# Graph layer kernel: the second join adds the base rows on GpSimd, and the last node stage reads one sum and stores the norms alone

## What is computed

```
xn = _layernorm(x, axis=-1)
x = x + _L0_gnn_ref(xn, edge_index, edge_attr_16, ...) + _L0_mix_ref(xn[None], ...)[0]
x = x + _L0_ffn_ref(_layernorm(x, axis=-1)[None], ...)[0]
return x
```

## Time and profile before

| | us |
|---|---|
| three runs | 3036.64, 3046.49, 3049.08 |
| median | 3046.49 |
| the profiled execution | 3039.37 |
| its span in the trace | 3037.6 |

### The profile page before, as it was taken

The page is one execution under the profiler, slowest core; times in us unless marked ns, Lnnn a source line. Parts: engine busy times, 40 slices in busy tenths (PEclk is TensorE's granted clock), DMA queues, the critical chain, the costliest instruction groups (busy, mean ns, idle before and its releaser), DMA issues. The chain is left out here.

```text
span 3037.6 us, 76113 instructions
## 1 busy us (share of the span) xinstructions
PE 2343.2 (77%) x15555; PEld 1937.5 (64%) x15556; DVE 2164.0 (71%) x6024; ACT 1172.0 (39%) x4767; POOL 1995.0 (66%) x2241
## 2 busy tenths in 40 slices
PE   6587878888888887847777777777777757499897
PEld 4466667676666666636666666666666536378786
DVE  7477878787877786647777778777787655666565
ACT  3244545444444444513333333333333442322222
POOL 4577777777777774577777777777777225166665
PEclk9799989999999999859988989898888857699999
DMA  9755655565555553256566556655555248444432
GB/s 255 207 169 156 172 157 166 166 171 160 166 168 168 157 167 86 86 146 180 159 178 175 168 169 175 176 167 173 172 169 167 62 140 271 121 160 152 122 116 86
DMA packets 295113, 484.48 MB, mean 159 GB/s; under 512 B 69669, under 2 KB 204989, under 8 KB 295045
## 3 DMA queue, kind: packets, MB, share of 16 engines
q0 software_dynamic: 96384, 286.92, 33.3%
q1 hardware_dynamic: 134340, 150.23, 17.1%
q10 hardware_dynamic: 64320, 46.56, 4.9%
HBM read 404.17 MB, written 81.43 MB: 160 GB/s over the span
## 5 line engine op out<-in xcount | busy, mean ns | idle before, releaser
L703 POOL DMA_INDIRECT e_rows<-table,e_idx x1664 | 1580.2, 950 | 557.1 <-issue 403.4
L1087 PE MATMUL e_ps_sum<-e_hot,e_msg 128*128 128x129 f32 x6656 | 1118.6, 306 | 267.3 <-DVE e_msg L744 210.6
L1087 PEld LDWEIGHTS e_ps_sum<-e_hot,e_msg 128*128 128x128 f32 x6656 | 920.9, 205 | 427.0 <-ACT parts L942 242.2
L941 ACT ACTIVATE acc<-e_ps_sum 128x256 f32 x1664 | 639.0, 384 | 1222.8 <-PE e_ps_sum L1087 1022.7
L744 DVE TENSOR_TENSOR e_msg<-e_rows,e_ps_pr 128x256 f32<-128x256 f32 x1664 | 654.6, 415 | 82.0 <-issue 12.9
L723 DVE TENSOR_TENSOR e_hot<-e_ps_pr,rel 128x512 f32<-128x512 f32 x416 | 285.4, 686 | 163.2 <-PE e_ps_sum L1087 157.7
L1069 PE MATMUL e_ps_al<-e_dst_score,e_hotT 128*128 x3328 | 301.6, 180 | 1.5 <-issue 0.7
L1069 PEld LDWEIGHTS e_ps_al<-e_dst_score,e_hotT 128*128 128x128 bf16 x3328 | 251.5, 99 | 60.1 <-issue 2.3
L942 ACT ACTIVATE parts<-e_ps_sum 128x4 f32 (+1 forms) x1664 | 280.4, 168 | 0.0
L1076 PE MATMUL e_ps_al<-ident,e_lr 128*128 128x128 f32 x104 | 38.6, 371 | 171.8 <-DVE e_lr L768 170.8
L2010 ACT ACTIVATE x_h<-x,eb 128x128 f32<-128x128 f32 x216 | 67.4, 363 | 260.8 <-PE x L2079 260.8
(11 more groups left out here) (319 smaller groups left out, 3400.4 us busy)
## 6 DMA issues: line engine op xcount, KB each, us to landing
e_relb<-rel_rows SPq DMA_DIRECT2D x104, 512.0 KB
e_rows<-table,e_idx POOLq DMA_INDIRECT x1664
e_eattr<-in_edge_b SPq DMA_DIRECT2D x104, 128.0 KB
e_xT<-turned_x ACTq DMA_DIRECT2D x100, 128.0 KB
e_xr<-in_x ACTq DMA_DIRECT2D x100, 128.0 KB
node<-acc SPq DMA_DIRECT2D x25, 512.0 KB, 3.8
table<-t_row SPq DMA_DIRECT2D x25, 276.0 KB, 4.1
table<-j_row SPq DMA_DIRECT2D x25, 276.0 KB, 2.5
```

Of the source, the lines that this page charges most:

```text
L703: nc.gpsimd.indirect_dma_start(out=rows[q][:, k, :], out_offset=None, in_=table, in_offset=bass.IndirectOffsetOnAxis(ap=idx[:, q, k:k + 1] ...
L941: nc.scalar.activation(acc[:, :, bass.ds(at[k], P)], ps_sum[(k + q) % 3][:, :, 0:P], ACT.Copy).then_inc(s["window"], 1)
L1087: op = nc.tensor.matmul(ps_sum[(k + q) % 3][:, a, 0:WIN], msg[:, k % RM, a * P:a * P + P], hot[:, q, k, :], start=(a == 0), stop=True, ski ...
```

## The change

The second join's result goes to the first 256 columns of `node` (row width 528) and no longer to a tensor `conv`, and what is stored there is already the sum with `base`:

- SyncE fetches the chunks of `base` into a new ring `part` of four, the first four ahead of all and then chunk n + 4 behind the store of chunk n.
- GpSimd adds `part` to `row` (128 x 512) behind each row copy. The store waits for this add.
- The base rows of the fix nodes are gathered by seven indirect DMAs at the head of GpSimd's program. VectorE adds them to `fix`, six blocks in one instruction and the last in another, and the scatters wait for these.

In `front` SyncE fetches one chunk of `node` straight into a slot of `xy`, now a ring of six (RX). There is no add. The fetch of chunk n + 4 is issued behind the store of chunk n and waits for the landing of the store of chunk n - 2. The store writes the second half of a slot only, 256 KB.

```diff
+            def fetch(n, q):
+                if layer == 1:
+                    sp.dma_start(part[:, q], base[bass.ds(n * CH, CH), :].rearrange("(b p) f -> p b f", p=P)
+                                 ).then_inc(s[f"part{q}"], 16)
...
+                for q in range(RR):
+                    store(RR * i + q, q)
+                    fetch(RR * i + RR + q, q)
...
+            if layer == 1:
+                def add(n, q, i):
+                    pool.wait_ge(s["rowc"], n + 3)
+                    pool.wait_ge(s[f"part{q}"], 16 * i + 16)
+                    pool.nop(nofuse=True)
+                    nc.gpsimd.tensor_tensor(row[:, q], row[:, q], part[:, q], ALU.add).then_inc(s["split"], 1)
+
+                for f in range(NFIX):
+                    n = min(P, T - f * P)
+                    nc.gpsimd.indirect_dma_start(
+                        out=fix_part[0:n, f, :], out_offset=None, in_=base,
...
+            else:
+                f, n = NFIX - 1, T - (NFIX - 1) * P
+                vec.wait_ge(s["fix_part"], 16 * NFIX)
+                vec.wait_ge(s["fixc"], f)
+                nc.vector.tensor_tensor(fix[:, 0:f], fix[:, 0:f], fix_part[:, 0:f], ALU.add).then_inc(s["fixs"], 1)
...
             def fetch(n):
-                if n >= 4:
-                    sp.wait_ge(s["x2"], n - 3)
-                sp.dma_start(bb[:, n % 4], base[n * CH:n * CH + CH, :].rearrange("(b p) f -> p b f", p=P)).then_inc(s[f"b{n % 4}"], 16)
-                sp.dma_start(cb[:, n % 4], conv[n * CH:n * CH + CH, :].rearrange("(b p) f -> p b f", p=P)).then_inc(s[f"c{n % 4}"], 16)
...
+                if n >= RX:
+                    sp.wait_ge(s[f"o{n % RX}"], 16 * (n // RX))
+                    sp.wait_ge(s["yt"], n - RX + 1)
+                sp.dma_start(xy[:, n % RX, :, 0:F], node[n * CH:n * CH + CH, 0:F].rearrange("(b p) f -> p b f", p=P)
+                             ).then_inc(s[f"x{n % RX}"], 16)
...
-                sp.dma_start(node[n * CH:n * CH + CH, 0:2 * F].rearrange("(b p) f -> p b f", p=P), xy[:, n % 3]
-                             ).then_inc(s[f"o{n % 3}"], 16)
...
+                sp.dma_start(node[n * CH:n * CH + CH, F:2 * F].rearrange("(b p) f -> p b f", p=P), xy[:, n % RX, :, F:2 * F]
+                             ).then_inc(s[f"o{n % RX}"], 16)
+                if n + RX - 2 < NCH:
+                    fetch(n + RX - 2)
...
-            for n in range(NCH + 1):
-                if n < NCH:
-                    pool.wait_ge(s[f"b{n % 4}"], 16 * (n // 4) + 16)
-                    pool.wait_ge(s[f"c{n % 4}"], 16 * (n // 4) + 16)
-                    if n >= 3:
-                        pool.wait_ge(s[f"o{n % 3}"], 16 * (n // 3))
-                        pool.wait_ge(s["yt"], n - 2)
-                    nc.gpsimd.tensor_tensor(xy[:, n % 3, :, 0:F], bb[:, n % 4], cb[:, n % 4], ALU.add).then_inc(s["x2"], 1)
```

More of the change, by code:

```diff
@@ L134, in build @@
             join(nc, sb, pb, sem, locals())
-        node = nc.dram_tensor("node", (NP, MW), F32).ap()
         mid = nc.dram_tensor("mid", (NP, MW), F32).ap()
@@ L1209, in join @@
     begins, sep, same = v["begins"], v["ends_sep"], v["ends_same"]
-    result = v["table"][1] if layer == 0 else v["conv"]
+    result = v["table"][1] if layer == 0 else v["node"]
+    base = v["base"]
     WIDTH = TW if layer == 0 else F
@@ L1248, in store @@
             def store(n, q):
-                sp.wait_ge(s["split" if layer == 0 else "rowc"], n + (1 if layer == 0 else 3))
-                sp.dma_start(result[bass.ds(n * CH, CH), :].rearrange("(b p) f -> p b f", p=P), row[:, q]
+                sp.wait_ge(s["split"], n + 1)
+                sp.dma_start(result[bass.ds(n * CH, CH), 0:WIDTH].rearrange("(b p) f -> p b f", p=P), row[:, q]
                              ).then_inc(s[f"out{q}"], 16)
-            with sp.Fori(0, ROUNDS) as i:
+            def fetch(n, q):
+                if layer == 1:
+                    sp.dma_start(part[:, q], base[bass.ds(n * CH, CH), :].rearrange("(b p) f -> p b f", p=P)
+                                 ).then_inc(s[f"part{q}"], 16)
+            for q in range(RR):
+                fetch(q, q)
+            with sp.Fori(0, ROUNDS - 1) as i:
                 for q in range(RR):
                     store(RR * i + q, q)
+                    fetch(RR * i + RR + q, q)
+            for q in range(RR):
+                store(NCH - 1 - RR + q, q)
+                if q == 0:
+                    fetch(NCH - 1, 0)
             store(NCH - 1, 0)
@@ L1272, in _ @@
                 nc.gpsimd.tensor_tensor(qs[:, 2, :], qs[:, 1, :], cst[:, 1:2].broadcast_to((P, NB)), ALU.pow)
+            if layer == 1:
+                def add(n, q, i):
[7 more added lines that the diff above has]
+                        out=fix_part[0:n, f, :], out_offset=None, in_=base,
+                        in_offset=bass.IndirectOffsetOnAxis(ap=fix_rows[0:n, f:f + 1], axis=0)).then_inc(s["fix_part"], 16)
+                with pool.Fori(0, ROUNDS) as i:
+                    for q in range(RR):
+                        add(RR * i + q, q, i)
+                add(NCH - 1, 0, ROUNDS)
             for q in range(RR):
@@ L1491, in front @@
     ident, cst, logits = v["ident"], v["cst"], v["logits"]
-    base, conv, node = v["base"], v["conv"], v["node"]
+    node = v["node"]
+    RX = 6
     with ExitStack() as ctx:
@@ L1514, in front @@
         ps_l = pb("f_l", [P, 512], ctx)
-        names = ("small", "b0", "b1", "b2", "b3", "c0", "c1", "c2", "c3", "o0", "o1", "o2", "x2", "mv", "rstd", "yn", "yt", "ytc",
+        names = ("small", *(f"x{q}" for q in range(RX)), *(f"o{q}" for q in range(RX)), "mv", "rstd", "yn", "yt", "ytc",
                  "rh", "rhc", "lg")
@@ L1554, in _ @@
+            for n in range(NCH):
+                pool.wait_ge(s["mv"], n + 1)
+                nc.gpsimd.tensor_tensor(rstd[:, n % 2], eps[:, n % 2], cst[:, 0:1].broadcast_to((P, 2)), ALU.pow
+                                        ).then_inc(s["rstd"], 1)
         @block.vector
```

35 lines of the change are left out of this document (15 added, 20 removed).

## The result

| | before | after |
|---|---|---|
| median, us | 3043.43 (4 runs, 3036.64 to 3049.08) | 3015.16 (4 runs, 3012.53 to 3016.59) |
| profiled execution, span | 3037.6 | 3010.7 |
| second join, VectorE's first scan to first scatter | 63.65 | 81.62 |
| last node stage, first fetch to logits | 102.84 | 58.22 |

The ratio is 0.9899, 95% interval 0.9884 to 0.9913: 28.3 us less, where 3017 and faster was forecast. The change is small, 1%, but the interval lies clear of 1. The spans differ by 26.9 us, and they add up: -2.5 (the join's first scan comes earlier), +18.0 (the join), +0.6 (scatters), -44.6 (the last node stage), +1.6 (all behind it).

A forecast was written before the change was run, and what follows sets the result against it. The prediction took the last node stage's three-deep ring as the limit there; front -43.1 and second join +15.7 give -27.4 us, from 3044.1 to about 3017 us, range 2999 to 3039.

The forecast's parts named there:

- Lock: Second join: GpSimd adds and VectorE scans block each other for the other's length; plus 15.7 us, without it only 3.1.
- tail: Second join's end: first scatter needs six copied fix rows and a VectorE add, not one copied row; 3.1 us more.
- The walk: Second join traced over the earlier rows, one add entering each gap between VectorE instructions: first scatter 15.7 us later.
- The gathers ... Nothing: Second join's start: seven gathers at 1.3 us take 9 us, done before the first row is copied; no cost.
- SyncE ... Nothing: Second join: 25 fetch issues of some 0.4 us in an almost empty queue, four rows ahead; no cost.
- L: Front: length of the first low-clock stretch, taken as 14 us; 25 steps take 46.8 + 0.46 L, 53.2 us.
- TensorE becomes the bound wherever the clock is low: Front: a TensorE step takes 3.47 us at the low clock, 1.87 at the high one, against VectorE's 1.87.
- the ring of three: Front before: a slot's store, landing, add, power and normalisation take 7.3 us for two steps and limit the stage.
- just hidden: Front: fetch landing of about 3 us plus 0.6 of issues is 3.6 against 3.74 us for two steps.
- B: Rival, second join: the adds hide, join +3.1 us, total change -40.0, 3004 us; chance 0.12.
- C: Rival, front: clock low for all 25 steps, front 93.3 us, total change +6.2, 3050 us; chance 0.14.
- D: Rival, front: fetch landing stays 4.2 us, a step 2.4, front 68.9, total change -18.2, 3026 us; chance 0.14.

The follow-up runs named there:

- no adds: Changed kernel without GpSimd's 25 adds in the second join, fetches and gathers kept: join 67.65 us, last row copied 59.21 us in, whole 3007.7 us.
- fills: Changed kernel with each of GpSimd's 25 second-join adds replaced by a fill of a scratch buffer that reads nothing: join 69.22 us, ratio to before 0.9900.
- the four profiles above: Unedited join profiled four times, once with the last node stage's fetch three steps ahead: 81.5 to 81.6 us three times, 79.08 us once.
- six slots: Kernel before with only the ring xy of the last node stage deepened from three slots to six: front 94.15 us, whole 3032.0 against 3046.3 us.
- The two other profiles with three held gathers: Two of the three unedited-join profiles near 81.6 us, with gathers held 4.04 to 4.21, 3.38 and 1.69 us.
- the pair of kernels: Changed kernel with TensorE adding base rows behind transposes, either both transposes of a bank opening a group or only the first: joins 67.66 and 67.74 us.

## Why the prediction held, and where its steps did not

**The total** was right within 2 us (3017 against 3015.2), and -27.4 for the profiled span against -26.9. Terms in it are wrong in ways that cancel, within `front` above all, so the closeness of the total is in part luck. So is the first scatter at 2489.89 where 2490.1 was forecast: the join's first scan came 2.5 us earlier than before.

**Join, +15.7 forecast, +18.0 and +15.4 measured.** Lock right in kind (no adds: 67.65; fills: 69.22). By place: L1479 +6.6 as forecast; last row +12.5 forecast, +14.0 and +11.4 measured; tail 3.1 forecast, 4.0 measured, so it was short by 0.9, since the fix copies come one behind the other before the six-block add of 1.76 us. The walk let one add in at every gap of VectorE. The trace shows more than one: what is queued runs through in a row (5.75 us for L1463). That the walk came out near in spite of this is partly luck. The last rows also pay for the fetches (below), which the walk had at nothing.

**"The gathers ... Nothing" failed.** I priced seven issues at 1.3 us and forgot that the gathers are themselves GpSimd instructions and can be held as the adds are: 4.04, 3.38 and 1.69 us. VectorE isn't held by them, so what they cost is the later and denser start of the adds. By the four profiles above this goes with the two joins, 81.6 and 79.1.

**"SyncE ... Nothing" failed in part.** Fetches by themselves cost nothing (59.21 without adds), but beside the adds they make the last rows 2.75 us later.

**Front, -43.1 forecast, -44.6 measured, by the wrong sum.** Start: 5.9 forecast, 6.4 measured. Steps: 1.87 forecast, 1.94 measured, with 2.0 us of waits for fetches. The low clock was charged 0.46 L, 6.4 us for L = 14. L was 7.4, and its price was zero: VectorE never waited for TensorE ahead of the logits, since with six slots TensorE may lag, and at the high clock it makes good (its transposes started at 2515.51 and 2517.21, 1.70 us a step against VectorE's 1.87). In the eleven profiles of the new `front` with the fetch four ahead L lay between 4.7 and 7.7 us; the longest went with a `front` of 58.09, the shortest with 60.12. What made up for part of it is the end: behind the last normalisation the last chunk passes transposes, two products and two copies, 4.86 us idle on VectorE before the logits, as the earlier trace rows already had it with 4.87. Behind the first matmul and 24 steps of 1.94 us, 5.2 us are left to the end of the logits, where I had one more step and 0.6, 2.5 us. So 59.7 goes to 58.2 by +0.5 (start), +1.7 (24 steps), -6.4 (low clock) and +2.7 (end), to a tenth or two. The step "TensorE becomes the bound wherever the clock is low" is refuted at this length of L; for a stage low throughout it wasn't tried.

**What bounded it before.** I named the ring of three, and put the queues below it. Both are so, but the queues lay just below: 8.7 of 44.6 us (six slots, 94.15). The forecast held because the change halves the bytes as well as deepening the ring.

**The landing** of the new fetches was put at about 3 us and "just hidden"; it is 3.1 by the median, and fetching one step later costs 18.2 us. The cycle was misdrawn, though: I had issues and landing against two steps, and the one that the rows show takes in moments and normalisation, over three.

**Rivals.** B (adds hide) fell: VectorE's products start 6.6 us late. C (clock low throughout) fell: 1.00 from 2515.5 on. D (landing 4.2) fell: 3.1.

## What to carry over

When a wait for a ring slot is the longest row, ask what the next limit is before giving the ring the credit: bytes per step over the measured rate is one line of arithmetic (1.05 MB at 345 GB/s is 3.0 us). Before work is moved to an idle GpSimd, look at what VectorE runs beside it: here scans and products with two SBUF operands and copies were stretched by GpSimd's adds, and they in turn held adds and indirect DMA issues. An add that rides on a PSUM accumulation kept clear of that here, but it cost TensorE time (a row copy every 1.6 us, not 1.33), and the join stayed 4.1 us longer than before the change. TensorE's slow start in the six-deep `front` cost nothing, since it caught up, while the way of the last chunk through all engines counted in full.

## What the runs showed of the hardware that I had not expected

- **An indirect DMA's issue is held by VectorE.** 0.95 us alone, 4.04 and 3.38 beside scans over 8 partitions, 1.69 beside a product, each until 0.76 to 0.80 us behind VectorE's end; in the kernel with fills as well (3.57 and 3.35), where no add was there. VectorE's scans beside them kept their 3.61 us.
- **Queued adds keep VectorE out as a series.** Adds of 1.24 us (three in 3.71): VectorE's product is recorded with 5.75 us in place of 1.88, until the fourth was done. The two other profiles with three held gathers have 5.65 and 5.71. Which engine wins when both are ready was not tried further.
- **Two transposes into one PSUM bank that each open a group spoil a sum added later.** Opened by the first alone the sum is whole. The Trainium skill (PSUM — Partial Sum Buffer, section The four PSUM rules) says that opening a group clears the marks of the whole bank and not the data; the pair of kernels agrees. Which columns were lost was not looked at.
- **The clock did not fall in the new `front`,** where TensorE was busy 9.9 to 10 us of 10 in the windows shown; before, it fell to 0.50 at about 2545.5, behind a window (2535 to 2545) with TensorE busy 4.0 us of 10, and it fell three times with six slots (PE busy 6.52 and 7.42 us of 10 in the two windows shown, at 0.96 and 0.75). Two chips granted only some 0.75 on average over the whole program (3964 and 3966 us); on the one where the changed kernel was repeated its ratio was the same.
